# Attention on stacked, rounded latents: one-pass key projections and maxima transpositions, and turns bank by bank

## The reference

```python
q = (x @ Wq + bq).reshape(B, T, H, D)
kv_latent = jax.nn.gelu(x @ Wkd + bkd, approximate=False)
lat = kv_latent[..., :L] + kv_latent[..., L:]
kv = lat @ Wku + bku
k = kv[..., :C].reshape(B, T, H, D)
v = kv[..., C:].reshape(B, T, H, D)
attn = jnp.einsum('bqhd,bkhd->bhqk', q, k) * scale
attn = jnp.where(causal, attn, -jnp.inf)
attn = jax.nn.softmax(attn, axis=-1)
out = jnp.einsum('bhqk,bkhd->bqhd', attn, v).reshape(B, T, C)
return out @ Wo + bo
```

## Time and profile before

| | |
|---|---|
| median of 3 runs | 646.83 us (646.17 to 647.59) |
| the profiled execution, its own time | 646.88 us |
| span of its trace | 645.0 us |
| TensorE matmul, busy | 599.1 us (93%), 3297 instructions |
| VectorE, busy | 542.1 us (84%), 1338 |
| ScalarE, busy | 487.6 us (76%), 858 |
| GpSimd, busy | 167.7 us (26%), 144 |
| chain that ended last, by engine | PE 63%, DVE 24%, ACT 6%, issue 4% |

### The profile page before, as it was taken

The page is one execution under the profiler, slowest core; times in us unless marked ns, Lnnn a source line. Parts: engine busy times, 40 slices in busy tenths (PEclk is TensorE's granted clock), DMA queues, the critical chain, the costliest instruction groups (busy, mean ns, idle before and its releaser), DMA issues.

```text
span 645.0 us, 10999 instructions
## 1 busy us (share of the span) xinstructions
PE 599.1 (93%) x3297; PEld 441.4 (68%) x3297; DVE 542.1 (84%) x1338; ACT 487.6 (76%) x858; POOL 167.7 (26%) x144
## 2 busy tenths in 40 slices
PE   8799889888999999999999999785898999999996
PEld 5466556555545688888888888354675888888884
DVE  4868888888858868988988888869799789999997
ACT  5658999999647899999999999798635556666663
POOL 4422323223304033553455342040432000000000
PEclk9899999999998999999999999996897999999998
DMA  7000000000100042112201210000000222222201
GB/s 252 1 1 3 1 3 1 1 0 1 34 1 0 6 164 99 52 47 99 98 29 68 98 49 1 1 1 1 0 1 2 69 91 89 91 90 90 91 0 67
DMA packets 6491, 28.83 MB, mean 45 GB/s; under 512 B 862, under 2 KB 990, under 8 KB 4383
## 3 DMA queue, kind: packets, MB, share of 16 engines
q1 hardware_dynamic: 6448, 28.32, 12.4%
HBM read 27.13 MB, written 1.19 MB: 44 GB/s over the span
## 4 chain that ended last, share of the span: by engine, by line
PE 63%; DVE 24%; ACT 6%; issue 4%; DMA 1%; POOL 0%; SPq 0%; DVEq 0%; ACTq 0%; POOLq 0%
PE PS L1213 17%; PE PS L1215 16%; PE PS L1214 16%; DVE STAT L874 9%; PE PS L1364 2%; PE PS L1292 2%; DVE RA L894 2%; PE PS L1319 2%; PE PS L1239 2%; DVE SU L900 1%; DVE HN L680 1%; PE PS L1333 1%; ACT STAT L397 1%; DVE HL L692 1%; ACT RA L635 1%
## 5 line engine op out<-in xcount | busy, mean ns | idle before, releaser
L1015 DVE TENSOR_TENSOR RA<-AR,RA 128x512 fp32r<-128x512 f32 x144 | 137.4, 978 | 26.2 <-ACT RA L518 24.6
L517 ACT ACTIVATE AR<-PS,BI 128x512 f32<-128x512 f32 x144 | 99.8, 693 | 15.3 <-PE PS L1215 7.8
L1213 PE MATMUL PS<-HH,WH 128*128 128x512 f32 x272 | 108.9, 400 | 0.2
L1215 PE MATMUL PS<-HL,WH 128*128 128x512 f32 x272 | 107.1, 394 | 0.0
L1214 PE MATMUL PS<-HH,WL 128*128 128x512 f32 x272 | 107.1, 394 | 0.0
L518 ACT ACTIVATE RA<-PS,BI 128x512 fp32r<-128x512 f32 x144 | 98.7, 685 | 0.0
L874 DVE CUSTOM_DVE_ANT_0 STAT<-PS,MQ 128x128 f32<-128x128 f32 (+1 forms) x256 | 76.3, 355 | 20.0 <-PE PS L1320 19.9
L1213 PE MATMUL PS<-RA,WH 128*128 128x512 f32 x208 | 83.0, 399 | 3.7 <-DVE RA L1179 2.1
L1215 PE MATMUL PS<-RA,WH 128*128 128x512 f32 x208 | 81.2, 391 | 0.0
L1214 PE MATMUL PS<-RA,WL 128*128 128x512 f32 x208 | 81.2, 391 | 0.0
L320 POOL TENSOR_TENSOR AR<-AR 128x512 f32<-128x512 f32 x32 | 50.8, 1587 | 113.2 <-DVE AR L827 113.2
(11 more groups left out here) (212 smaller groups left out, 1164.3 us busy)
## 6 DMA issues: line engine op xcount, KB each, us to landing
AR<-comb SPq DMA_DIRECT2D x15, 1024.0 KB, 4.7
WS<-in_w SPq DMA_DIRECT2D x9, 512.0 KB, 5.5
WS<-in_w SPq DMA_DIRECT2D x7, 384.0 KB, 3.1
M<-in_mats SPq DMA_DIRECT2D x1, 1384.0 KB, 10.8
X<-in_xT SPq DMA_DIRECT2D x4, 256.0 KB, 4.4
out_xT<-X SPq DMA_DIRECT2D x4, 256.0 KB, 2.1
AR<-in_wmod SPq DMA_DIRECT2D x1, 768.0 KB, 7.8
AR<-in_w SPq DMA_DIRECT2D x1, 384.0 KB, 3.1
```

Source lines behind the costliest of these rows:

```text
L517: act.activation(G[:, c, :], PS[:, c, :], ACT.Gelu_apprx_tanh, bias=bias).then_inc(s["act"], 1)
L1015: dve.tensor_tensor(out=GL[:, m0 % 2, c, :], in0=G[:, c, :], in1=f(GH[:, m0 % 2, c, :]), op=ALU.subtract).then_inc(s["lo"], 1)
L1213: pe.matmul(out, wh, xh, start=first, stop=False)
L1215: return pe.matmul(out, wh, xl, start=False, stop=last)
```

## The change

- **Selection instead of a plain latent.** ScalarE's gelu goes to LG (float32). A new matmul `three_rows` (98 outputs, 512 columns, float32, four of them) stacks the sum of both latent halves three times, with two rows of ones. VectorE's new `latents` turns that into a stack of rounded and rest parts (two instructions per block). The weights are split in the same way: KMR and KMS, 640 columns by VectorE ahead of the copy of the modulation, 512 columns by GpSimd.
- **One-pass projections.** Keys and values are then one float32r product of 98 rows each, and the bias of the queries is a second such product in the same accumulation. ScalarE's evacuation has no bias any more, and its two rounded copies are one instruction of 512 columns.
- **One-pass transposition.** `maxima_t` multiplies with a float32r identity IDR instead of a float32 transposition.
- **Bank by bank.** `scores` signals each bank by itself and waits for the maxima of that bank alone; `maxima` finishes bank 0 before bank 1.
- **LL moved.** The subtraction for LL goes on GpSimd from the start to behind the last rounding of hidden states before the experts of layer 0.
- `kmats` grows from 65x640 to 98x1250 numbers; KM moves from its own tile into AR.

```diff
-        LAT = AR[0:65, 8192:10240]
+        LG = AR[0:65, 8192:10240]
+        KM = AR[0:98, 2048:3298]
+        IDR = RA[:, 7936:8064]
+        LAT = RA[0:98, 3072:5120]
+        KMS = RA[0:98, 5120:6272]
+        KMR = RA[0:98, 6272:7424]
...
# gpsimd, start
+            qb = KM[:, 640:1152].rearrange("p (h r c) -> p h r c", r=4, c=8)
+            gp.tensor_scalar(qb[:, :, 0, :], qb[:, :, 0, :], -1.0, 0.0, ...).then_inc(qk_bias, 1)
+            gp.tensor_scalar(qb[:, :, 2:4, :], qb[:, :, 2:4, :], -1.0, 0.0, ...).then_inc(qk_bias, 1)
+            gp.tensor_scalar(KMR[:, 640:1152], KM[:, 640:1152], vec("w_sign")[0:98, :], ...).then_inc(qk_bias, 1)
+            gp.tensor_scalar(KM[:, 640:1152], KM[:, 640:1152], vec("w_keep")[0:98, :], ...).then_inc(qk_bias, 1)
+            gp.tensor_tensor(out=KMS[:, 640:1152], in0=KM[:, 640:1152], in1=f(KMR[:, 640:1152]), op=ALU.subtract)\
+              .then_inc(qk_bias, 1)
...
-            gp.wait_ge(l1_split, 1)
-            gp.wait_ge(hn_done, 8)
-            gp.tensor_tensor(out=LL[:, :], in0=lm, in1=f(LH[:, :]), op=ALU.subtract).then_inc(l1_split, 1)
...
             split_hidden(1, HN, 3)
+            gp.wait_ge(l1_split, 1)
+            gp.tensor_tensor(out=LL[:, :], in0=lm, in1=f(LH[:, :]), op=ALU.subtract).then_inc(l1_split, 1)
             experts(0, E0, 1024)
...
# scalar, evac_proj
-                act.activation(QKT[:, 0, :], PS[:, 6, 0:256], ACT.Identity,
-                               bias=KEPT[:, g:g + 1], scale=vec("q_keep")).then_inc(qk_evac, 1)
-                act.activation(QKR[:, 0, :], PS[:, 6, 0:256], ACT.Identity,
-                               bias=SIGNED[:, g:g + 1]).then_inc(qk_evac, 1)
+                act.activation(QKT[:, 0, :], PS[:, 6, 0:256], ACT.Copy, scale=vec("q_keep")).then_inc(qk_evac, 1)
                 act.activation(QKT[:, 1, :], PS[:, 6, 256:512], ACT.Copy, scale=vec("k_keep")).then_inc(qk_evac, 1)
-                act.activation(QKR[:, 1, :], PS[:, 6, 256:512], ACT.Copy).then_inc(qk_evac, 1)
+                act.activation(QKR[:, :, :], PS[:, 6, :].rearrange(...), ACT.Copy).then_inc(qk_evac, 2)
...
# vector
+            dve.wait_ge(flipped, 2)
+            dve.tensor_scalar(KMR[:, 0:640], KM[:, 0:640], vec("w_sign")[0:98, :], ...).then_inc(kms_done, 1)
+            dve.wait_ge(kms_done, 1)
+            dve.scalar_tensor_tensor(out=KMS[:, 0:640], in0=KM[:, 0:640], ...).then_inc(kms_done, 1)
...
+            def latents(t):
+                dve.wait_ge(sel_psum, t + 1)
+                if t >= 1:
+                    dve.wait_ge(l_done, t)
+                dve.tensor_scalar(LATR, PS[0:98, t, :], vec("lat_sign")[0:98, :], ...).then_inc(lr_done, 1)
+                dve.wait_ge(lr_done, t + 1)
+                dve.scalar_tensor_tensor(out=blk(LAT, t), in0=PS[0:98, t, :], ...).then_inc(l_done, 1)
...
             def maxima(n, n0, h):
-                dve.wait_ge(s_done, 2 * n + h + 1)
-                for q, (first, width) in enumerate(((0, 128), (128, 256))):
-                    for j in range(2):
+                for j in range(2):
+                    dve.wait_ge(s_done, 4 * n + 2 * h + j + 1)
+                    for q, (first, width) in enumerate(((0, 128), (128, 256))):
...
# tensor, project
-                pe.matmul(PS[:, 6, 0:256], mat("wq", g), HN[:, cols], start=True, stop=True)
-                pe.matmul(PS[:, 6, 256:512], KM[:, 128 * g:128 * g + 128], LAT[:, cols], start=True, stop=True)\
+                pe.matmul(PS[:, 6, 0:256], mat("wq", g), HN[:, cols], start=True, stop=False)
+                pe.matmul(PS[:, 6, 0:256], KMS[:, 640 + 128 * g:768 + 128 * g], LAT[:, cols], start=False, stop=True)
+                pe.matmul(PS[:, 6, 256:512], KMS[:, 128 * g:128 * g + 128], LAT[:, cols], start=True, stop=True)\
...
# tensor, scores
-                    if n0 >= 1:
-                        pe.wait_ge(max_done, 4 * n)
-                else:
-                    pe.wait_ge(max_done, 4 * n + 2)
                 for j in range(2):
+                    if h == 1:
+                        pe.wait_ge(max_done, 4 * n + 1 + j)
+                    elif n0 >= 1:
+                        pe.wait_ge(max_done, 4 * n - 1 + j)
...
-                mm.then_inc(s_done, 1)
+                      .then_inc(s_done, 1)
...
# tensor, maxima_t
-                    mm = pe.transpose(PS[:, 7, 256 + 128 * q:384 + 128 * q], f(MP[:, q, :]), IDF[:, :])
+                    mm = pe.matmul(PS[:, 7, 256 + 128 * q:384 + 128 * q], MP[:, q, :], IDR, start=True, stop=True)
...
# tensor, start
+            def three_rows(t):
+                pe.wait_ge(lat_done, t + 1)
+                pe.matmul(PS[0:98, t, :], KM[0:65, 1152:1250], blk(LG, t), start=True, stop=True).then_inc(sel_psum, 1)
+            for t in range(3):
+                latent(t)
+            three_rows(0)
+            latent(3)
+            three_rows(1)
+            three_rows(2)
...
             project(0, 0, 0)
+            three_rows(3)
```

More of the change, by code:

```diff
@@ L1282, in _, with latent @@
             pe.wait_ge(in_mats, 16)
-            for t in range(NBLK):
+            def latent(t):
                 pe.wait_ge(hn_done, 2 * t + 2)
@@ L1667, in layouts @@
     put("bo", a["L0_attn_bo"])
-    put("bq", heads(a["L0_attn_bq"], 3).T)
-    put("q_sign", np.array([1, -1, 1, 1], f4)[row])
     put("q_keep", np.array([0, 1, 0, 0], f4)[row])
@@ L1681, in layouts @@
     put("bkd", a["L0_attn_bkd"])
+    put("w_sign", np.repeat(np.array([-1, -1, 1, -1, 1], f4), [32, 32, 32, 1, 1]))
+    put("w_keep", np.repeat(np.array([0, 0, 1, 0, 1], f4), [32, 32, 32, 1, 1]))
+    put("lat_sign", np.repeat(np.array([-1, 1, -1, -1], f4), [32, 32, 32, 2]))
+    put("lat_keep", np.repeat(np.array([0, 1, 0, 0], f4), [32, 32, 32, 2]))
     put("c", np.concatenate([a["L0_c"], a["L1_c"]]).T)
@@ L1704, in layouts @@
         mats=mats,
-        kmats=np.concatenate([wk, wk, np.concatenate([bk.reshape(1, 512), np.zeros((1, 128), f4)], 1)]),
+        kmats=np.concatenate([np.concatenate([wk, wk, wk, bias, bias]), qb, pick], 1),
         rows=np.tile(rows, (128, 1)),
```

62 lines of the change are left out of this document (42 added, 20 removed).

## The result

| | median us | lowest to highest | profiled execution | span |
|---|---|---|---|---|
| before | 646.69 (4 runs) | 646.17 to 647.59 | 646.88 | 645.0 |
| changed | 652.38 (4 runs) | 651.15 to 652.92 | 651.15 | 649.2 |

The changed kernel is slower: ratio 1.0084, 95% interval 1.0064 to 1.0104, 5.7 us. The forecast was 644.2 in a range of 639.5 to 649.3; the prediction was wrong.

The account below looks back on a forecast made before the run. In the attention units no engine was saturated; a loop of waits through several engines, with VectorE's 0.60 us hole, set the pace. Units -7.6, start +2.0, moved subtraction +3.0 made -2.6 us: 644.2 us, range 639.5 to 649.3.

Parts of the forecast that it names:

- The way behind the last normalising instruction, +0.8: Start, from last normalising instruction to first scores: 7.4 us instead of 6.6, a loss of 0.8 us.
- First units, -1.3: First three units: two shorter evacuations and two shorter projections each save 1.3 us.
- GpSimd against VectorE, +1.5: Start: five more GpSimd instructions block VectorE, costing 1.5 us, between 0 and 4.5.
- Rival 2: At the start GpSimd holds VectorE for all it has: start +5.0, total 647.2 us; chance 0.15.
- VectorE's new instructions ahead of the copy, +1.0: Start: two 98x640 VectorE operations, 1.55 us, ahead of the modulation copy delay it by 1.0 us.
- LL, +3.0, bound 3.7: Expert stage start, layer 0: moved GpSimd subtraction holds VectorE and TensorE waits, costing 3.0 us (0 to 3.7).
- The unit, -7.6: Steady attention units: 4.13 us instead of 4.40, bound by TensorE; 0.27 us gained in each of 28, 7.6 in all.
- t+3.02: Steady unit, t being the start of `with_max`: the projection begins at t+3.02 as before.
- at t+1.61 as before: Steady unit, t being the start of `with_max`: bank 1's scores of h=1 start no later, its wait hidden.
- The transposition, 0: Steady unit: one-pass transposition of the maxima gains nothing, bounds -0.1 to +0.1; counting passes would give 0.32 us per unit.
- Rival 3: Attention units: TensorE's way round is the loop, unit falls by only 0.09 us, total 649.3 us; chance 0.15.

Follow-up runs that it names:

- h3: Changed kernel, LL back at the start behind GpSimd's first sum, GpSimd held behind normalising, alpha instructions late, eight more filling matmuls: 642.26 us, 0.9927.
- h2: Changed kernel, LL at the start behind GpSimd's first sum, GpSimd held, alpha late, one VectorE instruction per latent block (rounding rest omitted): 644.6 us, 0.9955.
- f1: Changed kernel with LL in its old place and GpSimd's four key-bias instructions held behind VectorE's eight normalising instructions: 644.46 us, 0.9940.
- i1: Kernel before with GpSimd held behind normalising, LL behind its first sum, and four filling matmuls ahead of the third projection: 645.84 us, 0.9975.
- f2: Changed kernel with LL in its old place and the float32 transposition of the paired maxima back: 649.12 us, 1.0034.
- e3: Kernel before with only the bank-by-bank turns of scores and maxima added: 648.10 us, 1.0011.
- e1: Changed kernel with the subtraction for LL back in its old place at the start: 648.65 us, 1.0029.

## Why the prediction was wrong

The mechanisms were nearly all there; the sizes at the start were not.

- **The way behind the last normalising instruction, +0.8: this step failed.** It measured +4.1. The sum took one pair of VectorE's instructions behind TensorE's last pass, as if the three pairs ahead were hidden. They were not: four pairs at 1.64 us, with 0.5 us of waiting after the first, are a row of 6.9 us, from 26.97 to 33.82, and TensorE's pass for block 0 stands in order behind its third latent. It also took full clock, where TensorE had been idle for 5.35 us: its fourth latent began 2.2 us behind the last normalising instruction, and 0.7 in h3, where the clock was up. The shares are about 1.3 for the second instruction (h2 against h3), 1.5 for the clock, and the remaining 1.3 for TensorE's added pass and order, which is argued and not tested.
- **First units, -1.3.** Measured +0.2, from scores to `with_max` 8.07 and 8.23 us. TensorE was at half clock for part of the stretch in both kernels (granted clock 0.59 from 32 to 36 us before, 0.50 and 0.66 from 36 to 44 now), longer in the changed one, and eight filling matmuls stand in front of the transposition there. So what the shorter evacuations saved was not on the way, or went to the clock; no run tells which. With the clock up the stretch takes 5.8 us (h3), and 6.5 in the kernel before (i1), 0.7 us more, where 1.3 was forecast.
- **GpSimd against VectorE, +1.5.** Measured +2.2 in the stretch, and 3.7 came back with the hold (f1). The step took half the GpSimd work as harmless; but it came in one row and one instruction waited for all of it. Rival 2 had this mechanism, with 647.2 us, and no rival had the step above.
- **VectorE's new instructions ahead of the copy, +1.0.** The copy came 0.51 us later, within the scatter of the start. The 1.55 us for the two instructions are less than the row named gives (2 x 0.69 x 640 / 512 is 1.7); they took 0.57 and 0.89.
- **LL, +3.0, bound 3.7.** Right in place, order and victim, and inside its bounds: 3.65 in the traces, 3.2 to 3.7 in time. The stall alone is the 3.0 forecast; what was missing is the clock behind it, which stayed low for some 4 us and cost 0.9. The Trainium skill, in SBUF — State Buffer (Who interferes with whom), has the exclusive port for the whole instruction; the 4.20 us beside 3.73 agree.
- **The unit, -7.6.** Measured -5.7, right in kind. Projection to transposition took 0.67 us (0.69 forecast) and from there 0.37 (0.42). But the projection began at t+3.17, not t+3.02: as the unit shrinks, the scores of h=0 no longer lie ready when `with_max` ends, the maxima begin at t+0.51 instead of t+0.36, and bank 1 and all behind it come 0.15 us later. That bank 1 would start "at t+1.61 as before" was the part that failed. It ran at t+1.77.
- **The transposition, 0**, in the bounds -0.1 to +0.1: 0.05 us a unit (f2). The Trainium skill's rule in TensorE: Matmul & The Clock Gate (Terms), float32 transposes four times faster in transpose mode, agrees.
- **Rival 3** asked whether TensorE's way round is the loop. It is with the turns alone (e3, 4.48 us on average); with both edits the unit fell to 4.25.

## What to carry to other kernels

When work is added in front of a stage, write out each engine's whole row there, not the last link: what comes once per block is hidden only if the row of it is shorter than its neighbour's. Put GpSimd's preparations behind the VectorE instructions on the way to the first result, for one of them can wait for a whole row of GpSimd's. And price a stall of TensorE with the slower clock behind it (here 0.9 us on a stall of 3.0), then look whether a few spare matmuls in the gap take that back. Before a difference of two traces is put down to one edit, look at a third that lacks only this edit: 0.9 of the 4.5 us between before and changed are there without the moved subtraction too (e1).
